# Attention in a three-stage decoder kernel: negated maxima straight into float16, reciprocals kept in PSUM, GpSimd's subtraction and ScalarE's exponentials cut in parts, slot arithmetic moved to the start

## The reference, cut to what matters

```python
x = layernorm(x + attention(x))                 # 4 x 256 tokens, D = 256, 16 heads of 16, causal
x = layernorm(x + experts_by_token_id(x))       # 4 experts, silu(x W) * (x W) then W
x = layernorm(x + router_ffn(x))                # 4 experts of width 1024, top 1

scores = einsum('bhqd,bhkd->bhqk', Q, K) / 4
attn = softmax(where(causal, -inf, scores))
out = einsum('bhqk,bhkd->bhqd', attn, V) @ o_proj.T
```

## Time and profile before

| | us |
|---|---|
| median of 3 runs (lowest to highest) | 351.31 (351.16 to 351.67) |
| span of the profiled execution, first to last instruction | 347.0 |
| busy: PE / DVE / ACT / POOL | 251.2 / 223.1 / 146.9 / 121.2 |
| mean granted TensorE clock | 0.866 of full |

### The profile page before, as it was taken

One profiled execution on the slowest core, in us unless ns is written; L12 is line 12 of the kernel. 1 busy time (PEld: TensorE's weight loads), 2 busy tenths in 40 slices (PEclk: granted clock), 3 DMA queues, 4 the chain that ended last, 5 costly groups with the idle time before them and its releaser, 6 DMA issues.

```text
span 347.0 us, 6126 instructions
## 1 busy us (share of the span) xinstructions
PE 251.2 (72%) x2079; PEld 172.5 (50%) x2096; DVE 223.1 (64%) x473; ACT 146.9 (42%) x202; POOL 121.2 (35%) x137
## 2 busy tenths in 40 slices
PE   3984767758668535644478963657999999999990
PEld 3553555546457424431266753223666665656670
DVE  4778689998998999458247775902345554444441
ACT  4341758577655656533246641003223333223210
POOL 8000243533663765936102235720022222222222
PEclk9999889889886885565879995669999999999997
DMA  7996162223132332615680000224000000000000
GB/s 222 338 318 190 24 221 62 64 61 95 55 98 62 83 103 60 184 36 176 174 327 2 3 0 12 92 67 122 2 15 17 1 12 15 15 15 7 10 7 14
DMA packets 17433, 29.34 MB, mean 85 GB/s; under 512 B 2044, under 2 KB 12926, under 8 KB 17408
## 3 DMA queue, kind: packets, MB, share of 16 engines
q1 hardware_dynamic: 15968, 25.84, 24.7%
q0 software_dynamic: 1440, 3.17, 2.6%
HBM read 19.69 MB, written 10.03 MB: 86 GB/s over the span
## 4 chain that ended last, share of the span: by engine, by line
PE 49%; DVE 25%; issue 11%; POOL 7%; DMA 3%; ACT 2%; SPq 0%; POOLq 0%; DVEq 0%; ACTq 0%
PE ps L1126 33%; DVE arena L842 4%; PE ps L1196 3%; POOL sorted L416 3%; PE ps L1429 3%; DVE arena L876 2%; DVE wf_lo L679 2%; PE ps L1192 2%; POOL sorted L453 2%; DVE arena L839 2%; PE ps L1132 2%; DVE arena L851 1%; POOL arena L430 1%; DVE arena L818 1%; DMA ring<-wqkvT 1%
## 5 line engine op out<-in xcount | busy, mean ns | idle before, releaser
L1126 PE MATMUL ps<-wf_hi,arena 128*128 x336 | 82.0, 329 | 2.7 <-DVE arena L1054 1.6
L430 POOL TENSOR_TENSOR arena<-arena 128x1536 f16<-128x1536 f32 (+1 forms) x16 | 51.2, 3203 | 72.8 <-ACT arena L532 68.3
L1126 PE MATMUL ps<-wf_lo,arena 128*128 x168 | 55.2, 328 | 0.0
L1126 PEld LDWEIGHTS ps<-wf_hi,arena 128*128 128x128 f16 x336 | 32.8, 98 | 26.9 <-issue 6.9
L632 ACT ACTIVATE arena<-ps 128x512 f32<-128x512 f32 x22 | 13.1, 597 | 65.2 <-PE ps L1126 65.2
L1054 DVE SCALAR_TENSOR_TENSOR arena<-ps,arena 128x512 f32<-128x512 f32 x22 | 15.2, 691 | 25.2 <-ACT arena L632 13.5
L527 ACT ACTIVATE arena<-ps 128x1536 f16<-128x1536 f32 x16 | 23.2, 1450 | 16.9 <-PE ps L1226 16.8
L459 POOL TENSOR_SCALAR veps<-mv 128x1 f32<-128x1 f32 x11 | 2.5, 225 | 79.0 <-DVE mv L1074 79.0
L1132 PE MATMUL ps<-wf_hi,ones 128*128 128x512 f16 x51 | 18.0, 523 | 12.0 <-DMA sorted<-arena,pos_i 5.2
L1126 PE MATMUL ps<-xT_hi,arena 128*128 x88 | 19.7, 289 | 5.8 <-DVE arena L1014 5.0
L532 ACT ACTIVATE arena<-ps 128x1536 f32<-128x1536 f32 x16 | 23.1, 1446 | 1.7 <-POOL arena L430 1.7
(11 more groups left out here) (202 smaller groups left out, 558.1 us busy)
## 6 DMA issues: line engine op xcount, KB each, us to landing
ring<-Wf SPq DMA_DIRECT2D x17, 512.0 KB, 3.7
sorted<-fill SPq DMA_DIRECT2D x1, 4515.0 KB, 23.3
arena<-Wf SPq DMA_DIRECT2D x7, 512.0 KB, 6.9
arena<-sorted SPq DMA_DIRECT2D x22, 129.0 KB, 2.1
sorted<-fill SPq DMA_DIRECT2D x1, 1419.0 KB, 9.5
ring<-xT SPq DMA_DIRECT2D x4, 256.0 KB, 5.0
X<-x_tok SPq DMA_DIRECT2D x1, 1024.0 KB, 7.8
ring<-ctxT SPq DMA_DIRECT2D x2, 512.0 KB, 3.8
```

The costliest lines, as they stand in the source:

```text
L430: g.tensor_tensor(Pl[n % 2][:, c], Pf[:, c], Ph[n % 2][:, c], ALU.subtract).then_inc(p_lo, 1)
L1126: last = t.matmul(dst, xs(k), ws(k), start=(k == 0 and m == 0), stop=(k == nk - 1 and m == 2))
```

## The change

- Row maxima: the reduction itself negates and writes float16 into one of two buffers (`Mn[b % 2]`). `negate`, the float32 buffer and the low part are gone; one extra row in place of two is transposed, copied and sent by DMA.
- Reciprocals go into a free part of PSUM bank 6, and one multiplication over both halves takes them from there. TensorE therefore waits for `o_norm` instead of `o_read` before it writes bank 6 again.
- GpSimd's subtraction of a step is three instructions, one for each bank; the first starts when the first bank's exponentials are done.
- ScalarE's exponentials of a step are four instructions (high and float32 of bank 3, then both of banks 4 and 5), and TensorE gives out bank 3 ahead of banks 4 and 5, and fills it again as soon as its two are done.
- The slot arithmetic runs before the first projection's low parts; to make room, GpSimd clears the second query buffer (`QT[1]`), which VectorE did.

```diff
@@ SyncE
-                    row = par * SLOT + 3 * DK
-                    src = par * 2 * PAIRS
-                    sp.dma_start(QT[b % 3][row:row + 2, par::2, :],
-                                 mT[src:src + 2 * PAIRS, :]).then_inc(m_row, 16)
+                    sp.dma_start(QT[b % 3][row:row + 1, par::2, :],
+                                 mT[par * PAIRS:(par + 1) * PAIRS, :]).then_inc(m_row, 16)
@@ GpSimd
-            pool.wait_ge(const_q2, 1)
+            link(g.memset(QT[1][SLOT:P, 0::2, :].bitcast(F32), 0.0))
+            g.memset(QT[1][0:SLOT, 1::2, :].bitcast(F32), 0.0).then_inc(const_q2, 1)
+            pool.wait_ge(const_q2, 2)
...
-                pool.wait_ge(exped, 2 * n + 2)
+                pool.wait_ge(exped, 4 * n + 2)
                 if n >= 2:
                     pool.wait_ge(av_rdy, n - 1)
-                c = slice(0, 3 if n < STEPS - 1 else 1)
-                g.tensor_tensor(Pl[n % 2][:, c], Pf[:, c], Ph[n % 2][:, c], ALU.subtract).then_inc(p_lo, 1)
+                g.tensor_tensor(Pl[n % 2][:, 0], Pf[:, 0], Ph[n % 2][:, 0], ALU.subtract).then_inc(p_lo, 1)
+                if n < STEPS - 1:
+                    pool.wait_ge(exped, 4 * n + 4)
+                    for c in range(1, 3):
+                        g.tensor_tensor(Pl[n % 2][:, c], Pf[:, c], Ph[n % 2][:, c], ALU.subtract).then_inc(p_lo, 1)
@@ ScalarE, exps
-                a.activation(Ph[n % 2], ps[:, 3:6, :], ACT.Exp, scale=DK ** -0.5).then_inc(exped, 1)
+                a.activation(Ph[n % 2][:, 0], ps[:, 3, :], ACT.Exp, scale=DK ** -0.5).then_inc(exped, 1)
                 if g == 1 and b >= 1:
                     o_hi(b - 1)
                 if n >= 1:
-                    act.wait_ge(p_lo, n)
-                a.activation(Pf, ps[:, 3:6, :], ACT.Exp, scale=DK ** -0.5).then_inc(exped, 1)
+                    act.wait_ge(p_lo, 3 * (n - 1) + 1)
+                a.activation(Pf[:, 0], ps[:, 3, :], ACT.Exp, scale=DK ** -0.5).then_inc(exped, 1)
+                act.wait_ge(st_rdy, 2 * n + 2)
+                a.activation(Ph[n % 2][:, 1:3], ps[:, 4:6, :], ACT.Exp, scale=DK ** -0.5).then_inc(exped, 1)
+                if n >= 1:
+                    act.wait_ge(p_lo, 3 * n)
+                a.activation(Pf[:, 1:3], ps[:, 4:6, :], ACT.Exp, scale=DK ** -0.5).then_inc(exped, 1)
@@ VectorE
-            for q in QT[0:2]:
...
+            v.memset(QT[0][SLOT:P, 0::2, :].bitcast(F32), 0.0)
+            v.memset(QT[0][0:SLOT, 1::2, :].bitcast(F32), 0.0).then_inc(const_z, 1)
+            x_low(1)
+            dve.wait_ge(cnt_sb, 1)
+            running()
+            slot_tiles(0, NT)
+            slots()
...
                 v.tensor_reduce(dst[:, 0], ps[:, 0, :].rearrange("p (a r k) -> p a r k", a=2, r=2),
-                                AX.X, ALU.max).then_inc(maxed, 1)
+                                AX.X, ALU.max, negate=True).then_inc(maxed, 1)
...
-                v.reciprocal(Or, o[:, :, 2 * DK])
+                inv_sum = ps[:, 6, 272:272 + TB * G]
+                v.reciprocal(inv_sum, o[:, :, 2 * DK])
...
-                for q in range(TB):
...
-                ins.then_inc(o_norm, 1)
+                v.tensor_tensor(dst, Oa.rearrange("p (q a) c -> p q a c", q=TB),
+                                inv_sum.rearrange("p (q a) -> p q a", q=TB).unsqueeze(3)
+                                .to_broadcast([P, TB, G, DK]), ALU.mult).then_inc(o_norm, 1)
...
-            negate(0)
...
-                if g == 2 and b + 1 < B:
-                    negate(b + 1)
...
-                if step == 3 * NG - 1:
-                    dve.wait_ge(cnt_sb, 1)
-                    running()
-                    slot_tiles(0, NT)
-                elif step == 3 * NG:
-                    slots()
@@ TensorE
-                pe.wait_ge(m_neg, b + 1)
+                pe.wait_ge(maxed, 2 * NG * (b + 1))
                 if b >= 1:
-                    pe.wait_ge(o_read, NG * b - 2)
+                    pe.wait_ge(o_norm, NG * b - 2)
...
-                if n >= 1:
-                    pe.wait_ge(exped, 2 * n)
                 for bank, kt, qt in ((3, 0, 0), (4, 0, 1), (5, 1, 1)):
+                    if n >= 1 and bank == 3:
+                        pe.wait_ge(exped, 4 * n - 2)
+                    elif n >= 1 and bank == 4:
+                        pe.wait_ge(exped, 4 * n)
...
-                last.then_inc(st_rdy, 1)
+                    if bank != 4:
+                        last.then_inc(st_rdy, 1)
...
-                pe.wait_ge(p_lo, n + 1)
+                pe.wait_ge(p_lo, 3 * n + (3 if n < STEPS - 1 else 1))
...
-                    pe.wait_ge(o_read, n)
+                    pe.wait_ge(o_norm, n)
```

More of the change, by code:

```diff
@@ L153, in build @@
         Oa = carve([TB * G, DK], F32)
-        Or = carve([TB * G], F32)
         OT_hi = carve([TB, NK, P], F16)
         OT_lo = carve([TB, NK, P], F16)
-        Mx = carve([TB, 2, PAIRS], F32)
-        Mn = carve([TB * 2, 2, PAIRS], F16)
+        Mn = [carve([TB, 2, PAIRS], F16) for _ in range(2)]
         mT = carve([S], F16)
@@ L378, in _ @@
             for j in range(2):
-                last = g.memset(Ks[j][:, :, 3, 0:2], 1.0)
+                last = g.memset(Ks[j][:, :, 3, 0:1], 1.0)
             last.then_inc(const_s, 1)
```

38 lines of the change are left out of this document (11 added, 27 removed).

## The result

| | before | after |
|---|---|---|
| median of 4 runs each (lowest to highest), us | 351.24 (350.18 to 351.67) | 330.69 (328.5 to 333.13) |
| span of the profiled execution, us | 347.0 | 326.4 |
| busy: PE / DVE / ACT / POOL, us | 251.2 / 223.1 / 146.9 / 121.2 | 244.8 / 205.6 / 147.8 / 131.1 |
| mean granted TensorE clock | 0.866 | 0.895 |

What follows compares the result with a forecast made beforehand. VectorE, partly standing still beside GpSimd's subtractions, was taken to bound most of attention. Terms -6.6 (steps 2 to 8), -5.4 (8 to 12), -3.0 (12 to 16) and -1.5 (start) sum to -16.5: 334.8 us, range 327.5 to 342.

Steps and rivals of the forecast that it cites:

- VectorE's standing still: Attention: two-SBUF-input VectorE instructions wait out GpSimd's subtractions; with reciprocals in PSUM the multiplication takes 0.28 us, and negations go.
- Where the wait goes next: Attention steps 2 to 12: VectorE's weight chunks meet GpSimd's pieces instead, 0.4 us each, 2.4 and 1.6 us.
- Rival (a): Attention: GpSimd's pieces keep the port, so the wait moves whole to the weight chunk; 340 us, chance 0.17.
- Steps 2 to 8: Attention: VectorE's busy time falls from 39.6 to 32.4 us; with 12% idle, 37.0 against 43.6 us, -6.6.
- some 85% as a sign: Attention steps 2 to 12: VectorE's busy share would fall to some 85% if the forecast was right.
- rival (c): Attention: idle stays at 9% and meetings of chunks with pieces are rare; 328.5 us, chance 0.15.
- Steps 8 to 12: Attention: ScalarE becomes the bound with 17.5 us busy; at 9% idle 19.2 against 24.6 us, -5.4.
- Slot arithmetic and steps 12 to 15: Late attention: without slot arithmetic, step 13's subtraction follows step 12's by 4.6 us, not 7.6: -3.0; GpSimd's chain afterwards stays.
- The start: First 57.6 us: a long VectorE instruction of 3.58 us meets pieces, not a whole subtraction; -1.5 us, between 0 and 2.9.
- Overhead of the pieces: GpSimd's subtraction in three: each piece costed at 3.10 / 3 = 1.03 us, with no overhead.
- The small waits: Three sequences in attention: VectorE idles perhaps 0.4 us each behind TensorE's transposes of maxima, counted in the idle share.
- What I expected not to move: Stages after attention keep their length, shifted by about 16 us; a change over 2 us would show the forecast wrong.

Runs made afterwards that it cites:

- u1: The changed kernel with its reciprocals back in SBUF, the single multiplication kept: 333.89 us, ratio 0.950 to the kernel before.
- d2: The kernel before with only the negation merged into the maxima reduction, which writes float16: 347.20 us, ratio 0.989 to the kernel before.
- d12: The kernel before with reciprocals in PSUM, one multiplication and the negation merged into the reduction: 338.31 us, ratio 0.963 to the kernel before.
- u2: The changed kernel with GpSimd's subtraction as one instruction behind all exponentials of its step: 339.72 us, ratio 0.968 to the kernel before.
- u4: The changed kernel with the slot arithmetic back in steps 11 and 12: 329.70 us, ratio 0.940 to the kernel before.
- d4: The kernel before with only the slot arithmetic moved to the start and QT[1] cleared by GpSimd: 350.89 us against 352.77, ratio 0.997.
- v1: The changed kernel with the scatters of the first two sequences moved behind the last subtraction: 326.55 us, ratio 0.930 to the kernel before.
- u3: The changed kernel with the exponentials back in two instructions of 1536 columns, subtraction still in three: 336.54 us, ratio 0.957 to the kernel before.
- v12: The changed kernel with first two sequences' scatters behind the last subtraction and weight chunks kept from GpSimd's descriptor writing: 324.16 us, ratio 0.916 to the kernel before.
- d1: The kernel before with only the reciprocals in PSUM and one multiplication: 344.21 us, ratio 0.981 to the kernel before.
- a2: The changed kernel run once more, unaltered: 330.63 us, ratio 0.937 to the kernel before.

## Why the prediction was right, and where its terms were not

**VectorE's standing still (right).** L873 takes 0.288 us in all 16 steps; I had taken 0.28. L851 and L852 are gone. The theory of an exclusive hold between VectorE's instructions with two SBUF operands and GpSimd's subtraction is shown by u1 (one operand moved, 288 to 608 ns) and by d2 (the wait handed on). With these two parts alone (d12), steps 2 to 8 go from 43.5 to 37.6 us and 8 to 12 from 24.7 to 20.2.

**Where the wait goes next (right in kind and size, short in reach).** I put 0.4 us on each of ten chunks, 4.0. The ten that VectorE splits between 58 and 109 us have 3.2 us over 1.21 (three of them a wait of about one piece, at 58.82, 89.32 and 107.25). Left out of the sum were the chunks of steps 13 and 14: the one at 110.67 has 0.75 more and the one at 115.68, 3.92, over the 2.3 us that I named as the most for a chunk. I also missed a second victim. Normalisation's tensor_scalar (L909), with one tensor operand and two scalars from SBUF, has a mean of 786 ns, against 408 in the kernel before:

```profile
L909 DVE TENSOR_SCALAR X<-X,mv,rstd 128x256 f32<-128x256 f32 x8 | 6.0, 786 | 2.5 <-POOL rstd L408 2.5
```

That is 3.0 us more, in two pairs (at 87.31 and 104.93, 2.09 and 2.40 us against 0.74) that began beside GpSimd's pieces. Rival (a), a whole wait on each chunk, is not what is seen in steps 2 to 12 (2.22 us at most there), and u2 shows what it would have cost.

**Steps 2 to 8: -6.6 forecast, -8.6 measured.** The busy time came out as worked (32.4 forecast, 32.54). What was off was the idle share: 12% forecast (by which 32.4 gives 36.8 us, not the 37.0 of the sum), (34.92 - 32.54) / 34.92 = 7% measured. So VectorE is 93% busy there, and 94% in steps 8 to 12, where I had named some 85% as a sign: it stayed the bound. ScalarE is 87% busy without holding VectorE up more than before. This is the busy side of the forecast with the idle side of rival (c).

**Steps 8 to 12: -5.4 forecast, -5.6 measured.** ScalarE was named as the bound; it is 16.56 of 19.10, 87%, but GpSimd is 17.51, 92%, and with the clock at 0.98 the stretch fits either reading. That the two terms agree doesn't show that ScalarE was it.

**Slot arithmetic and steps 12 to 15: -3.0 forecast, -2.4 measured, and the agreement is luck.** This step failed in both its parts. I had read the 7.6 us between the subtractions of steps 12 and 13 as VectorE's lateness through the slots, with 4.6 left; 3.4 are left, 4.2 less. The slots' place is 2.0 of that (u4 has 5.4), and 1.9 come without moving them (d12 has 5.7). And I had put the chain from step 13 to 15 down as GpSimd's own, which stays at 12.7 us. It grew to 15.2: step 13's pieces stand still for 2.0 us beside two chunks, step 14's issues take 1.80 and 1.54 us against 1.00 and 0.97, and the pieces have their overhead, while step 13's first issue is 1.0 us shorter. So the two errors nearly cancel. For the whole kernel u4 and d4 tell no gain from the slots' place. What bounds the stretch now is GpSimd's list, as v1 shows. The size of the moved work was right (2.9 us for 14 instructions, 3.1 forecast): the mistake was to take for critical what stood beside an engine that was late anyway.

**The start: -1.5 forecast, -6.4 and -3.9 measured.** The mis-sized step. L929 begins with GpSimd's pair at 39.52 and runs first (0.69 us against 3.58; the pair waits, 2.82 against 2.27), so all of its 2.9 us is gained where I took one or two rests off; and I had costed the cut of the exponentials at 0.3 us a step with nothing bought, while ScalarE's start on the first bank alone saves it 0.9 us of idle time in step 0 (u3). Seven executions end step 2 between 54.3 and 57.8, against 60.7: 2.9 to 6.4 us. The one at 54.3 had the highest clock, 1.00 from 22 to 60 us; u1 and v12 had 0.91, as the kernel before had, and end at 56.9 and 57.8. So some 3 to 4 us are the change's, and still over twice the forecast. That the first profile showed more is luck.

**The cuts work only as a pair.** With d12 as the base (0.963), the exponentials cut but not the subtraction gives 0.968 (u2), the subtraction cut but not the exponentials 0.957 (u3), both 0.945 and 0.937. Alone each is within 2 us of nothing, together they are worth 6 to 9. In steps 2 to 8 it is otherwise: there the cut subtraction alone gives all of it (d12 37.6, u3 34.8, the change 34.9), and the exponentials' cut pays at the start and in steps 8 to 12. That GpSimd's first piece must be allowed to begin early, and then be over soon, is how I read it; no run shows the link. (u2 and u3 also have the slots early, which by u4 and d4 makes no difference that can be told.)

**Overhead of the pieces: none forecast.** A step's three pieces take 1.16 + 2.27 = 3.43 us against 3.10: 0.33 for two more instructions. The Trainium skill, GPSIMD Engine Reference, section Elementwise — side-by-side cycle accounting, gives about 156 ns of dispatch per instruction for VectorE, and for GpSimd no figure, only one software hop more. What the trace shows for GpSimd is 0.17 us for each added piece, against my zero; over fifteen steps it is 5.0 us of GpSimd's time, of which only what falls in GpSimd's own stretch, from step 12 on, counts in full.

**The small waits.** Behind the transposes of maxima VectorE idles 0.85, 0.85 and 0.46 us, where I had 0.4 each and let the idle share carry it; that share came out below my 12% all the same.

**What I expected not to move.** The second stage is 2.3 us longer, over the 2 us that I named as a sign of a wrong forecast. VectorE, ScalarE and GpSimd do the same work in it (38.79 against 38.86 us, 24.18 against 24.30, 22.44 against 22.43); TensorE is busy 46.66 against 44.06 at a granted clock of 0.75 against 0.79. So no engine but TensorE does more, and no added wait shows. But the clock isn't shown as the cause either: the stage takes some 67.7 us in d1 (0.75) and 67.0 in d2 (0.78), 68.0 in a2 (0.73) and 65.5 in u3 (0.77). It differs by 2 to 3 us from one execution to the next, whatever the kernel, and the 2.3 lie within that. The sign was too sharp for one trace of each.

In the sum, -4.9 at the start and -2.0 in steps 2 to 8 were gained beyond the forecast, 0.6 less came in steps 12 to 15, and 2.3 were given back later. The mechanism was right and the sum good to 4.1 us, helped by errors of both signs.

## What to carry to other kernels

A busy engine may be standing still: lay the durations of one line beside the other engine's timeline before costing its work. Taking one such wait away hands it to the next instruction of the kind in the same list, so remove them all, or cut the other side's instruction and let its first piece begin early. And before crediting work moved out of a stretch, ask which engine's list is the chain there, and test the move by itself. Cutting two traces at the same events shows where a gain lies; a repeat of the same kernel shows how much of it is one execution's.
